# Turns of the identity ahead of three waits of TensorE in a four-layer transformer kernel

## The chip, the cores and the metric

The kernel runs on one core of one Trainium2 chip. The metric is the device time of one execution in microseconds, the median of the runs taken. The core has a matrix engine (TensorE, PE in the profile, with PEld for its weight loads), a vector engine (VectorE, DVE), an activation engine (ScalarE, ACT), GpSimd (POOL) and SyncE (SP), which starts the transfers. Each engine runs its own instructions in order and waits for the others by semaphores.

## The reference, cut to what matters

The activations x have the shape (2, 2048, 256) in float32. Four layers follow one another, each added to its input: an attention with 16 heads, a mixture, an attention by distance, and the same mixture again.

```python
x = x + attn_a(layernorm(x))                    # causal, 16 heads of 16
x = x + ffn(layernorm(x), Wr, W1, b1, W2, b2)
x = x + attn_b(layernorm(x), Wq, bq, Wk, bk, Wv, bv, Wo, bo)
x = x + ffn(layernorm(x), Wr, W1, b1, W2, b2)

def ffn(x, Wr, W1, b1, W2, b2):                 # 8 experts, the best 2 per batch
    top_scores, top_idx = top_k(x.mean(axis=1) @ Wr, 2)
    weights = softmax(top_scores)
    h = gelu(einsum('btd,bkdf->bktf', x, W1[top_idx]) + b1[top_idx])
    y = einsum('bktf,bkfd->bktd', h, W2[top_idx]) + b2[top_idx]
    return einsum('bk,bktd->btd', weights, y)

def attn_b(x, ...):                             # q, k, v are x @ W + b
    dist_sq = q_sq[:, :, None] + k_sq[:, None, :] - 2.0 * einsum('bqd,bkd->bqk', q, k)
    return einsum('bqk,bkd->bqd', softmax(exp(-dist_sq)), v) @ Wo + bo
```

## The kernel before

x stays on the core for the whole kernel, as 32 tiles of 128 rows. The work goes in stages: head attention, mixture 0, the weights of the distance attention, the distance attention, mixture 1. Between them stands a barrier of all engines, in most cases with a clearing of the stage's semaphores (`end_stage`, L106). A stage is written as one program for each engine; nothing plans it, the order within an engine is the order of the code.

A "turn" is a transpose on TensorE: a weight load and a matmul against the 128 x 128 identity, from on-chip memory into a bank of PSUM. Four turns bring two tiles of normed x into columns. A product in full precision is made of three matmuls, since each operand is split into a high and a low part: `split_product` (L634 to L636) multiplies high by high, low by high and high by low, 512 columns each.

**A mixture** (`mixture`) works on two batches of four chunks of 512 rows. A step is one of 2 experts x 8 slices of 128 hidden units: an "up" product of 6 matmuls (L634 to L636, into `f_h`), ScalarE's gelu (L912), VectorE's scaling by the gate and split into high and low (L983, L985), and a "down" product of 6 matmuls into `yps` (`f_ypsum`), three steps behind the up. The list `before` sets the head of the stage. All engines go through the same 14 entries in order and each does its part: 0 and 1 norm (VectorE, L606), 2 and 3 turn (TensorE, L617; ScalarE then copies the high part, L623), 4 and 5 low (VectorE, L628), 6 tanh (ScalarE, L893), 7 gate (VectorE, L945), 8 spread of the gates over the partitions (TensorE, L826), 9 gates (VectorE, L949), 10 turn of the biases (TensorE, L832), 11 biases (VectorE, L953 to L959, waits for entry 10), 12 and 13 the first two parts of the weights (ScalarE L902, then VectorE L965). TensorE's first up waits for VectorE's entry 12. Its third up (up 2) needs the third part of the weights, which ScalarE and VectorE make beside step 0, behind gelu 0. SyncE loads the raw weights from the start of the stage, in eight transfers of 512 KB, and for the first batch waits for nobody on TensorE.

**The distance attention** (`distance_attention`) begins with turns 0 and 1 (L1213), the projection (0, 0) and (0, 1) of q, turn 2, the projections (1, 0) and (1, 1) of k, the lengths, turn 3 and the values. The first projection needs the low halves of turns 0 and 1 (VectorE, L1468, behind ScalarE's high halves, L1349). `outs` are the four banks of the projections and results, of which bank 0 is first written for real by projection (0, 0). ScalarE takes each projection out twice (L1363 the value, L1366 its square). The 128 steps behind this head are scores, two exponentials and weighted values.

Of the kernel before, what the change touches and what calls it, by code (L numbers as in the profile page):

```python
# [40 lines left out]
P = 128  # L41
# [15 lines left out]
class Program:  # L57
# [36 lines left out]
    def ps(self, ctx):  # L94
        return lambda name, shape, dt: ctx.enter_context(self.nc.psum_tensor(name, shape, dt))
# [91 lines left out]
class Routing:  # L187
# [49 lines left out]
    def choose(self, dve):  # L237
        pr, b = self.pr, self.b
        dve.wait_ge(self.s_logit, 1)
        dve.tensor_copy(pr.logits[:], self.bank[0:1, 0:E]).then_inc(self.s_logits, 1)  # L240
        dve.wait_ge(self.s_logits, 1)
        dve.max(pr.best[:], pr.logits[:]).then_inc(self.s_best, 1)
        dve.wait_ge(self.s_best, 1)
        dve.max_index(pr.best_i[:, b, :], pr.best[:], pr.logits[:]).then_inc(self.s_chosen, 1)
        dve.tensor_tensor(pr.lead[0:1, b:b + 1], pr.best[0:1, 0:1], pr.best[0:1, 1:2], ALU.subtract).then_inc(self.s_chosen, 1)


def load_batch(pr, sp, b):
# [383 lines left out]
def split_product(pe, out, fixed_hi, fixed_lo, moving_hi, moving_lo, first, last):  # L632

    pe.matmul(out, fixed_hi, moving_hi, start=first, stop=False)  # L634
    pe.matmul(out, fixed_hi, moving_lo, start=False, stop=False)  # L635
    return pe.matmul(out, fixed_lo, moving_hi, start=False, stop=last)  # L636
# [35 lines left out]
def mixture(pr, layer, last_layer):  # L672
# [5 lines left out]
    with ExitStack() as ctx:  # L678
# [19 lines left out]
        yps = ps(f"{st}_ypsum", [P, 2 * KD, CHUNK], F32)  # L698
# [30 lines left out]
        def beside(n):  # L729
# [29 lines left out]
            if at < WP - ahead:  # L759
# [4 lines left out]
        before = [("norm", (0, 0)), ("norm", (0, 1)), ("turn", (0, 0)), ("turn", (0, 1)), ("low", (0, 0)), ("low", (0, 1)),  # L764
                  ("tanh", 0), ("gate", 0), ("spread", 0), ("gates", 0), ("turn_biases", 0), ("biases", 0)]
        before += [("weights", (0, i)) for i in range(AHEAD)]

        with nc.Block() as block:
# [30 lines left out]
            @block.tensor  # L799
            def _(pe):  # L800
                use = [0]
                side_reads = []

                def side_free():
                    for s_read, count in side_reads:
                        pe.wait_ge(s_read, count)
                    side_reads.clear()

                def do(kind, what):
                    if kind == "turn":  # L810
                        side_free()
                        cols.turn(pe, use[0])
                        use[0] += 1
                        return
                    if kind == "sums":
                        pe.wait_ge(cols.s_lo, use[0])
                        side_free()
                        routing.sums(pe)
                    elif kind == "logits":
                        routing.products(pe)  # L820
                        side_reads.append((routing.s_logits, 1))
                    elif kind == "spread":
                        pe.wait_ge(s_gate, what + 1)
                        pe.wait_ge(cols.s_lo, use[0])
                        side_free()
                        pe.matmul(side[:, 0:TOPK], pr.ones[0:1, :], gate[0:1, 4:4 + TOPK], start=True, stop=True).then_inc(s_spread, 1)  # L826
                        side_reads.append((s_gates, what + 1))
                    elif kind == "turn_biases":
                        pe.wait_ge(s_braw, 4 * 16 * (what + 1))
                        pe.wait_ge(cols.s_lo, use[0])  # L830
                        side_free()
                        pe.transpose(side[:, 0:BR], brow[:], pr.ident[0:BR, 0:BR]).then_inc(s_bturn, 1)  # L832
                        side_reads.append((s_bcol, what + 1))

                def up(n):
                    q, c, e, j = steps[n]
                    if c == 0:
                        pe.wait_ge(s_wl, WP * q + 8 * e + 2 * (j // 2) + 1)
                    if e == 0 and j == 0:
                        pe.wait_ge(cols.s_lo, (TILES // 2) * q + 2 * (c + 1))  # L840
                    if n >= 2:
                        pe.wait_ge(s_gelu, n - 1)
                    for k in range(KD):
                        mm = split_product(pe, hps[:, n % 2, :], w1h[:, e, k, j * P:(j + 1) * P], w1l[:, e, k, j * P:(j + 1) * P],
                                           cols.hi[:, k, c * CHUNK:(c + 1) * CHUNK], cols.lo[:, k, c * CHUNK:(c + 1) * CHUNK],
                                           k == 0, k == KD - 1)
                    mm.then_inc(s_h, 1)

                def down(n):
                    q, c, e, j = steps[n]  # L850
                    chunk = CHUNKS * q + c
                    if c == 0:
                        pe.wait_ge(s_wl, WP * q + 8 * e + 2 * (j // 2) + 2)
                    if e == 0 and j == 0 and chunk >= 2:
                        pe.wait_ge(s_y, KD * (chunk - 1))
                    pe.wait_ge(s_hl, n + 1)
                    for k in range(KD):
                        mm = split_product(pe, yps[:, KD * (chunk % 2) + k, :], w2h[:, e, j, k * P:(k + 1) * P],
                                           w2l[:, e, j, k * P:(k + 1) * P], hh[:, n % HR, :], hl[:, n % HR, :],
                                           e == 0 and j == 0, e == TOPK - 1 and j == FT - 1)  # L860
                    mm.then_inc(s_used, 1)

                for work in before:
                    do(*work)
                for n in range(len(steps) + LAG):
                    if n < len(steps):
                        up(n)
                    if n >= LAG:
                        down(n - LAG)
                    chunk, at = divmod(n, CS)  # L870
                    if 1 <= chunk < NB * CHUNKS and at in (4, 6):
                        add_tensor(pe, chunk - 1, (at - 4) // 2, ysb, s_y)
                    if n < len(steps):
                        for work in beside(n):
                            do(*work)
                for half in range(2):
                    add_tensor(pe, NB * CHUNKS - 1, half, ysb, s_y)
# [188 lines left out]
def distance_attention(pr, w):  # L1066
# [11 lines left out]
    with ExitStack() as ctx:  # L1078
# [24 lines left out]
        outs = ps("d_outs", [P, 2 * KD, CHUNK], F32)  # L1103
# [64 lines left out]
        def turn_bank(kind, p):  # L1168

            return {("turn", 1): banks[:, 0, :], ("turn", 2): banks[:, 1, :], ("values", 0): banks[:, 1, :]}.get((kind, p), turns[:])  # L1170
# [23 lines left out]
        with nc.Block() as block:  # L1194
            @block.tensor
            def _(pe):
# [7 lines left out]
                def turn(p):  # L1204
                    bank = turn_bank("turn", p)
                    if p not in (1, 2):
                        free(turn_read)
                        turn_read.append((s_xlo, p + 1))
                    pe.wait_ge(s_xn, 2 * p + 2)
                    out = bank.rearrange("p (k n) -> p k n", k=KD)  # L1210
                    for i in range(2):
                        for k in range(KD):
                            mm = pe.transpose(out[:, k, i * P:(i + 1) * P], xn[:, (2 * p + i) % 4, k * P:(k + 1) * P], pr.ident[:])  # L1213
                    mm.then_inc(s_turn, 1)
# [16 lines left out]
                def project(i, m):  # L1231
                    kind, g = tasks[i]
                    pe.wait_ge(s_xlo, 2 * g + 2)
                    if i in (7, 8, 14, 15):
                        pe.wait_ge(s_y, KD * {7: 1, 8: 3, 14: 4, 15: 5}[i])
                    elif i >= 2:
                        pe.wait_ge(s_lo, KD * (i - 1) + m + 1)
                    first = (2 * g % XR) * 2 * P
                    for k in range(KD):
                        mm = split_product(pe, outs[:, BANKS[i] + m, :], w.hi[kind][:, k, m * P:(m + 1) * P],  # L1240
                                           w.lo[kind][:, k, m * P:(m + 1) * P], xhi[:, k, first:first + CHUNK],
                                           xlo[:, k, first:first + CHUNK], k == 0, k == KD - 1)
                    mm.then_inc(s_p, 1)
# [63 lines left out]
                    mm.then_inc(s_rturned, 1)  # L1307

                do = {"turn": turn, "values": values, "project": project, "lengths": lengths}
                turn(0)  # L1310
                turn(1)
                project(0, 0)
                project(0, 1)
                turn(2)
# [5 lines left out]
                for n in range(STEPS + LAG):  # L1320
# [4 lines left out]
                    chunk, at = divmod(n, TILES)  # L1325
# [293 lines left out]
```

## Time and profile before

| what | value |
|---|---|
| median of 3 runs | 1852.38 us (1851.29 to 1853.46) |
| the profiled execution, its own time | 1851.4 us |
| its span, first to last instruction | 1849.4 us |
| TensorE busy | 1733.3 us, 94% of the span, 10063 matmuls |
| VectorE, ScalarE, GpSimd busy | 57%, 53%, 19% of the span |
| mean granted TensorE clock | 0.983 of full speed |

The profile is of one execution. Its times count from the first instruction; "granted clock" is the share of TensorE's full speed that the chip gave it, 1.00 for 2.4 GHz and 0.50 for 1.2 GHz. The ends of matmuls are modelled. A row's idle time is the time in which that engine did nothing ahead of the instruction, with the instruction that ended the wait.

### The profile page before, as it was taken

The page shows a single profiled execution, that of the slowest core. Times are in us where ns is not written, and L with a number is a line of the kernel's source. Part 1 is how long each engine was busy: PE and PEld are TensorE (multiplying, and loading weights), DVE is VectorE, ACT ScalarE, POOL GpSimd, SP SyncE. Part 2 cuts the span into 40 slices and gives each one's busy share as a digit, 9 for nine tenths or more (in the row PEclk, how much of TensorE's full clock was granted, in tenths as well). Part 3 has the DMA queues.
Part 4 walks back from the last instruction along what each step waited for, and adds up shares of the span by engine and source line. Part 5 has one row for each costly group of instructions (what it writes and reads, how often), then busy time and mean ns, then how long its engine had stood idle before and what let it go on. Part 6 is the DMA issues. An engine that isn't in the chain of part 4 may idle for free. (4 is left out here: it accounts for less than half of the span.)

```text
span 1849.4 us, 27445 instructions
## 1 busy us (share of the span) xinstructions
PE 1733.3 (94%) x10063; PEld 1138.5 (62%) x10063; DVE 1057.1 (57%) x2225; ACT 972.4 (53%) x1372; POOL 356.5 (19%) x466
## 2 busy tenths in 40 slices
PE   4999999999997999999998999999999799999998
PEld 1222222222222888888877887788788588888886
DVE  5443423444412775675546677865876587567554
ACT  3899999999996322332214544454444342233221
POOL 2222222232220000000003443533444200000000
PEclk9999999999998999999998999999999899999999
DMA  3000000000002002000000000000000200300000
GB/s 114 1 1 1 1 1 1 2 1 1 1 1 83 10 1 91 1 1 1 0 1 1 1 1 1 1 1 1 1 1 1 85 7 1 114 12 12 12 12 23
DMA packets 22912, 28.01 MB, mean 15 GB/s; under 512 B 1191, under 2 KB 18686, under 8 KB 22782
## 3 DMA queue, kind: packets, MB, share of 16 engines
q1 hardware_dynamic: 22782, 26.27, 4.3%
q8 instruction: 82, 1.34, 0.3%
q14 instruction: 48, 0.39, 0.1%
HBM read 22.07 MB, written 4.19 MB: 14 GB/s over the span
## 5 line engine op out<-in xcount | busy, mean ns | idle before, releaser
L449 ACT ACTIVATE a_probs<-a_scores 128x1024 f32<-128x1024 f32 (+3 forms) x640 | 513.0, 948 | 63.1 <-PE a_scores L549 61.3
L912 ACT ACTIVATE f_gelu<-f_h,f_bcol 128x512 f32<-128x512 f32 x256 | 176.6, 690 | 465.9 <-PE f_h L636 462.8
L527 PE MATMUL a_out<-a_probs,a_values 128*32 128x512 f32 (+3 forms) x2560 | 302.6, 545 | 4.4 <-POOL a_probs L472 4.3
L983 DVE TENSOR_SCALAR f_hh<-f_gelu,f_gates 128x512 fp32r<-128x512 f32 x256 | 124.3, 486 | 242.0 <-ACT f_gelu L912 240.8
L549 PE MATMUL a_scores<-a_moving,a_fixed 64*128 64x512 f16 (+3 forms) x1280 | 195.5, 355 | 29.8 <-ACT a_probs L449 22.4
L634 PE MATMUL f_h<-f_xhi,f_w1h 128*128 128x512 f32 x512 | 208.5, 407 | 11.3 <-DVE f_w1l L965 11.3
L1399 ACT ACTIVATE d_score<-d_dist,d_nksq 128x512 f32<-128x512 f32 x128 | 92.8, 725 | 213.7 <-DVE d_dist L1543 213.7
L636 PE MATMUL f_h<-f_xhi,f_w1l 128*128 128x512 f32 x512 | 202.2, 395 | 0.0
L635 PE MATMUL f_h<-f_xlo,f_w1h 128*128 128x512 f32 x512 | 201.8, 394 | 0.0
L634 PE MATMUL f_ypsum<-f_hh,f_w2h 128*128 128x512 f32 x512 | 199.8, 390 | 0.0
L636 PE MATMUL f_ypsum<-f_hh,f_w2l 128*128 128x512 f32 x512 | 199.5, 390 | 0.0
L635 PE MATMUL f_ypsum<-f_hl,f_w2h 128*128 128x512 f32 x512 | 199.4, 389 | 0.0
L985 DVE SCALAR_TENSOR_TENSOR f_hl<-f_gelu,f_gates,f_hh 128x512 fp32r<-128x512 f32 x256 | 192.4, 752 | 9.2
L549 PEld LDWEIGHTS a_scores<-a_moving,a_fixed 64*128 64x128 f16 x1280 | 47.7, 94 | 230.7 <-ACT a_probs L449 194.1
L1439 POOL TENSOR_TENSOR distance_raw<-distance_raw,d_p 128x512 f32<-128x512 f32 x112 | 145.4, 1298 | 201.0 <-ACT d_p L1373 200.9
L472 POOL TENSOR_SCALAR_AFFINE_SELECT a_probs<-a_probs 128x256 f32<-128x256 f32 x256 | 101.1, 410 | 247.3 <-ACT a_probs L449 243.4
L1543 DVE SCALAR_TENSOR_TENSOR d_dist<-d_banks,d_qsq 128x512 f32<-128x512 f32 x128 | 88.0, 687 | 63.6 <-PE d_banks L636 63.4
L634 PEld LDWEIGHTS f_h<-f_xhi,f_w1h 128*128 128x128 f32 x512 | 97.7, 191 | 31.3 <-DVE f_w1l L965 13.1
L636 PEld LDWEIGHTS f_h<-f_xhi,f_w1l 128*128 128x128 f32 x512 | 97.5, 190 | 21.3
L527 PEld LDWEIGHTS a_out<-a_probs,a_values 128*32 128x32 f32 x2560 | 50.6, 108 | 97.0 <-issue 83.0
L635 PEld LDWEIGHTS f_h<-f_xlo,f_w1h 128*128 128x128 f32 x512 | 98.0, 191 | 18.2
L636 PEld LDWEIGHTS f_ypsum<-f_hh,f_w2l 128*128 128x128 f32 x512 | 96.3, 188 | 20.4
(186 smaller groups left out, 2613.7 us busy)
## 6 DMA issues: line engine op xcount, KB each, us to landing
f_raw<-in_L_ffn_W SPq DMA_DIRECT2D x32, 512.0 KB, 7.5
x<-in_L_attn_a_x SPq DMA_DIRECT2D x8, 512.0 KB, 7.2
out<-x SPq DMA_DIRECT2D x8, 512.0 KB, 2.9
distance_raw<-in_L_attn_b_Wv SPq DMA_DIRECT2D x1, 256.0 KB, 7.0
distance_raw<-in_L_attn_b_Wo SPq DMA_DIRECT2D x1, 256.0 KB, 6.5
distance_raw<-in_L_attn_b_Wq SPq DMA_DIRECT2D x1, 256.0 KB, 6.6
distance_raw<-in_L_attn_b_Wk SPq DMA_DIRECT2D x1, 256.0 KB, 6.5
f_brow<-in_L_ffn_b SPq DMA_DIRECT2D x8, 4.0 KB
```

The lines of the kernel that those rows point to most:

```text
L449: act.activation(probs[:, u % UR, :, 0:w], scores[:, 2 * (u % SR):2 * (u % SR) + 2, 0:w], ACT.Exp, scale=HD ** -0.5).then_inc(s_exp, 1)
L472: pool.affine_select(out=tri, in_=tri, compare_op=ALU.is_ge, fill=0.0, base=0, pattern=[[0, 2], [1, P]], channel_multiplier=-1).then_inc(s ...
L527: mm = pe.matmul(spare[32 * j:32 * j + 32, i % 2, skip:CHUNK], values[:, G % 2, kt, j, :], probs[:, (2 * n + j // 2) % UR, j % 2, 0:w], st ...
L549: mm = pe.matmul(scores[:, 2 * (u % SR) + h, 0:w], fixed[head, G % 2, a, kt * P:(kt + 1) * P], moving[head, G % 2, a, q0:q0 + w], start=Tr ...
L634: pe.matmul(out, fixed_hi, moving_hi, start=first, stop=False)
L635: pe.matmul(out, fixed_hi, moving_lo, start=False, stop=False)
L636: return pe.matmul(out, fixed_lo, moving_hi, start=False, stop=last)
L912: act.activation(gel[:, n % HR, :], hps[:, n % 2, :], ACT.Gelu, bias=bcol[:, q, FT * e + j:FT * e + j + 1])\
L983: dve.tensor_scalar(hh[:, n % HR, :], gel[:, n % HR, :], gates[:, q, e:e + 1], None, ALU.mult).then_inc(s_hh, 1)
L985: dve.scalar_tensor_tensor(out=hl[:, n % HR, :], in0=gel[:, n % HR, :], scalar=gates[:, q, e:e + 1], in1=hh[:, n % HR, :].bitcast(F32), op ...
L1399: act.activation(score[:, n % 2, :], dist[:, n % DR, :], ACT.Exp, scale=-1.0, bias=nksq[:, b, kt:kt + 1]).then_inc(s_score, 1)
L1439: pool.tensor_tensor(acc, acc, p32[:, n % R, :], ALU.add).then_inc(s_acc, 1)
```

## The change

A new helper, `idle_turns`, issues a number of turns of the identity into a bank. It waits for nothing and signals nothing. In each mixture TensorE issues 20 such turns ahead of entry 0 of `before`, 20 ahead of entry 9 (so between the spread and the turn of the biases), and 24 behind the list, ahead of the first up. They go into bank 0 of `yps`, which the first down product starts anew. In the distance attention it issues 14 ahead of turn 0 and 12 between turn 1 and the first projection, into bank 0 of `outs`, which that projection starts anew. The result is the same.

```diff
--- before.py
+++ after.py
@@ -243,6 +243,12 @@
         dve.wait_ge(self.s_best, 1)
         dve.max_index(pr.best_i[:, b, :], pr.best[:], pr.logits[:]).then_inc(self.s_chosen, 1)
         dve.tensor_tensor(pr.lead[0:1, b:b + 1], pr.best[0:1, 0:1], pr.best[0:1, 1:2], ALU.subtract).then_inc(self.s_chosen, 1)
+
+
+def idle_turns(pr, pe, bank, count):
+
+    for _ in range(count):
+        pe.transpose(bank[:, 0:P], pr.ident[:], pr.ident[:])
 
 
 def load_batch(pr, sp, b):
@@ -860,8 +866,11 @@
                                            e == 0 and j == 0, e == TOPK - 1 and j == FT - 1)
                     mm.then_inc(s_used, 1)
 
-                for work in before:
+                for at, work in enumerate(before):
+                    if at in (0, 9):
+                        idle_turns(pr, pe, yps[:, 0, :], 20)
                     do(*work)
+                idle_turns(pr, pe, yps[:, 0, :], 24)
                 for n in range(len(steps) + LAG):
                     if n < len(steps):
                         up(n)
@@ -1307,8 +1316,10 @@
                     mm.then_inc(s_rturned, 1)
 
                 do = {"turn": turn, "values": values, "project": project, "lengths": lengths}
+                idle_turns(pr, pe, outs[:, 0, :], 14)
                 turn(0)
                 turn(1)
+                idle_turns(pr, pe, outs[:, 0, :], 12)
                 project(0, 0)
                 project(0, 1)
                 turn(2)
```

## Rows read from the trace of the kernel before

**Rows 1.** The page, parts 1 and 2: busy times, granted clock in 40 slices.
```profile
PE 1733.3 (94%) x10063; PEld 1138.5 (62%) x10063; DVE 1057.1 (57%) x2225; ACT 972.4 (53%) x1372; POOL 356.5 (19%) x466
...
PEclk9999999999998999999998999999999899999999
```

**Rows 2.** Timeline, first mixture's head: start us, us, engine, line, operation, [idle before].
```profile
585.70 1.38 DVE L606 TENSOR_SCALAR f_xn<-x,mv,rstd 128x256 f32<-128x256 f32 x4 [0.99 <-PEq L106]
586.49 0.66 PE L617 MATMUL f_side<-ident,f_xn 128*128 128x128 f32 x4 [2.99 <-DVE f_xn L606]
587.14 1.03 PE L617 MATMUL f_misc<-ident,f_xn 128*128 128x128 f32 x4
...
589.67 0.55 PE L826 MATMUL f_side<-f_gate,ones 1*128 1x2 f32 x2 [1.50 <-DVE f_gate L945]
...
594.34 0.80 PE L634 MATMUL f_h<-f_xhi,f_w1h 128*128 128x512 f32 x1 [3.51 <-DVE f_w1l L965]
...
597.35 1.28 ACT L912 ACT_TABLE_LOAD   x1 [2.15 <-PE f_h L636]
...
601.62 0.79 PE L634 MATMUL f_h<-f_xhi,f_w1h 128*128 128x512 f32 x1 [2.79 <-DVE f_w1l L965]
```

**Rows 3.** One-microsecond windows, first mixture: length, busy times; PEclk third from last.
```profile
587.00:588.00 1.00, 1.00 (x6) 0.63 (x4) 0.27 (x2) 0.60 (x1) 0.00 (x0) 0.64 0.00 0
...
597.00:598.00 1.00, 1.00 (x5) 0.74 (x4) 0.00 (x0) 0.65 (x1) 0.00 (x0) 0.74 1.02 370
...
600.00:601.00 1.00, 0.00 (x0) 0.00 (x0) 1.00 (x3) 0.95 (x2) 0.00 (x0) 0.96 1.05 378
...
607.00:608.00 1.00, 1.00 (x4) 0.76 (x3) 0.64 (x2) 0.85 (x2) 0.00 (x0) 0.62 0.00 0
```

**Rows 4.** Timeline in narrow windows: two turns at full, two and three at low clock.
```profile
586.49 0.44 PE L617 MATMUL f_side<-ident,f_xn 128*128 128x128 f32 x2 [2.99 <-DVE f_xn L606]
...
1464.74 0.69 PE L617 MATMUL f_side<-ident,f_xn 128*128 128x128 f32 x2 [2.79 <-DVE f_xn L606]
...
1464.74 0.90 PE L617 MATMUL f_side<-ident,f_xn 128*128 128x128 f32 x3 [2.79 <-DVE f_xn L606]
```

**Rows 5.** Timeline, head of the distance attention.
```profile
979.37 2.20 DVE L1463 TENSOR_SCALAR d_xn<-x,mv,rstd 128x256 f32<-128x256 f32 x4 [0.32 <-PEq L1012]
...
980.16 1.12 PE L1213 MATMUL d_turns<-ident,d_xn 128*128 128x128 f32 x4 [1.88 <-DVE d_xn L1463]
...
981.62 1.12 PE L1213 MATMUL d_banks<-ident,d_xn 128*128 128x128 f32 x4 [0.35 <-DVE d_xn L1463]
...
984.15 0.80 PE L634 MATMUL d_outs<-d_xhi,wq_hi 128*128 128x512 f32 x1 [1.41 <-DVE d_xlo L1468]
...
989.44 0.79 PE L1213 MATMUL d_banks<-ident,d_xn 128*128 128x128 f32 x3
```

**Rows 6.** One-microsecond windows, head of the distance attention.
```profile
979.00:980.00 1.00, 0.00 (x0) 0.00 (x0) 0.68 (x3) 0.00 (x0) 0.14 (x1) 0.90 0.00 0
...
990.00:991.00 1.00, 1.00 (x7) 0.87 (x6) 0.00 (x0) 1.00 (x3) 0.00 (x0) 0.98 0.00 0
```

**Rows 7.** Timeline, head of the second mixture.
```profile
1464.74 1.12 PE L617 MATMUL f_side<-ident,f_xn 128*128 128x128 f32 x4 [2.79 <-DVE f_xn L606]
...
1468.22 0.55 PE L826 MATMUL f_side<-f_gate,ones 1*128 1x2 f32 x2 [1.50 <-DVE f_gate L945]
...
1472.27 0.80 PE L634 MATMUL f_h<-f_xhi,f_w1h 128*128 128x512 f32 x1 [2.89 <-DVE f_w1l L965]
...
1479.55 0.49 PE L634 MATMUL f_h<-f_xhi,f_w1h 128*128 128x512 f32 x1 [1.80 <-DVE f_w1l L965]
...
1482.40 0.39 PE L634 MATMUL f_ypsum<-f_hh,f_w2h 128*128 128x512 f32 x1
```

**Rows 8.** One-microsecond windows, head of the second mixture.
```profile
1461.00:1462.00 1.00, 0.95 (x4) 0.55 (x4) 0.01 (x1) 0.00 (x0) 0.00 (x0) 0.54 0.00 0
...
1478.00:1479.00 1.00, 0.00 (x0) 0.00 (x0) 1.00 (x3) 1.00 (x2) 0.00 (x0) 0.92 1.05 375
```

## The prediction

> **What bounds the kernel now.** The page comes first: TensorE is busy for 94% of the span, and its granted clock dips in only a few of the forty slices [rows 1]. In the long middle of each stage one matmul follows another, so a delay or a gain at a stage's head reaches the end of the kernel almost whole, and the change can only matter at three heads. I read those with two views: the timeline, for who starts when, and the one-microsecond windows, for the granted clock. Times such as 586.49 are microseconds from the span's start.
>
> At the head of the first mixture the reader is to see short pieces of work that wait for VectorE and for the weights: two groups of four turns, the spread of the gates, and only at 594.34 the first product (up 0), then a wait to 601.62 before up 2 [rows 2]. The clock falls to half speed (1.2 GHz) at about 587.3. It rises to 2.4 GHz at about 597.5, falls again at about 600.9 and rises at about 607.8 [rows 3]. At the distance attention's head the clock falls at 979.8 and rises at 990.0 [rows 6], over the first twelve projections, which take 5.3 us from 984.15 to 989.44 [rows 5], 0.44 each. At full speed twelve products take 2.85, from 1479.55 to 1482.40 [rows 7], 0.24 each. Before the second mixture it has fallen at 1461.1, ahead of the stage, and rises at 1478.1 [rows 7, 8].
>
> What half speed costs there, as a ceiling: products run in it for 3.2 and 6.1 us in the first mixture, 5.9 in the distance attention, and 5.5 in the second mixture (1472.27 to 1477.75, where the 1.80 us of idle time ahead of 1479.55 begin). Full speed would halve each, 10.3 us in all. That is the most there is to win.
>
> **The price of one turn.** Two turns take 0.44 us and four take 0.66 at the full clock, so a further one costs 0.11. At the low clock two take 0.69 and three 0.90, so 0.21 [rows 2, 4]. Twenty cost 2.2 or 4.2 us, 24 cost 2.6 or 5.0, 14 cost 1.5 or 2.9, 12 cost 1.3 or 2.5. The change adds 2 x 64 + 26 = 154 turns. All stand in TensorE's own order, in front of real work, so each turn beyond the pause it stands in makes that work late. Nobody reads the bank before its first real write, which starts it anew, so nobody waits for the turns themselves.
>
> **First mixture.** When TensorE comes out of the stage's barrier isn't shown. The bounds are 585.70, VectorE's first instruction, and 586.49, TensorE's own first [rows 2]; I take 586.0. The pause that the first 20 turns are to fill is then 0.5 us. Twelve run before the clock falls at 587.3, as it did, and 8 at 0.21, so they end at 589.0. The eight real turns follow, a group of four at 1.1 us and one at 0.9, and end near 591.0 against 588.17, so 2.8 late. ScalarE's copies, VectorE's lows, the tanh and the gate hang on them, so the spread moves from 589.67 to 592.5. Behind it come 20 turns, the turn of the biases, and 24 turns, before up 0. VectorE's wait for the biases now stands behind the first 20, and VectorE makes its first half of the weights only after that wait; even so this half comes before the 24 have ended, so the turns are what is late. Those 44 take 4.8 us at the full clock. From the low clock it depends on when the clock rises: the four stretches of products above saw it rise 3.2, 5.9, 5.8 and 6.1 us after they began. With 3.2 the 44 take 15 x 0.21 + 29 x 0.11 = 6.4; with 6.1 they take 29 x 0.21 + 15 x 0.11 = 7.8. I take 6.4, between the others. With 0.7 for the spread (0.55 [rows 2]) and the one turn of the biases, up 0 starts at 599.6, 5.3 late (3.7 to 6.7). It then runs at full speed and is done after 1.55 us (6 x 0.24 and the end of the last) instead of 3.0 (from 594.34 to ScalarE's table load at 597.35 [rows 2]), which gives back 1.45. What follows is a chain: table load, gelu 0, VectorE's next weights, up 2 at 601.62. It is not shortened, so it starts 3.8 later. Up 1 ends with the same pause of some 3 us behind it, in which the clock fell before. I take the same fall again, so nothing is gained there; the other end is a clock that holds, for half of 6.1 us. First mixture: **+3.8**, from -0.9 to +5.2.
>
> **Distance attention.** VectorE starts at 979.37, and I let TensorE go into its 14 turns at 979.4. The clock fell at 979.8. TensorE had then been idle since 978.28, of the 1.88 us ahead of its first turn [rows 5, 6]. The pause shrinks to 1.1. The nearest row is the pause of 1.80 us ahead of 1479.55, over which the clock stood at full speed [rows 7, 8], so I take it that it holds. Turn 0 then starts at 980.9, 0.75 late, but takes 0.66 for 1.12, and ends at 981.6 against 981.28. Turn 1 ends at 982.2 against 982.74. The twelve turns end at 983.5, just ahead of the low halves, due 1.4 us behind turn 1 as before, at 983.6. So they are hidden, and the projections start at 983.6 for 984.15. The twelve projections take 2.85 us for 5.3, and turn 2 comes at 986.5, 2.9 early. ScalarE and VectorE, which copy each projection as it ends, follow it. **-2.9**. The ends are -3.2 (half of 5.3, and the 0.55 of the earlier start), and +2.4 if the clock is low throughout and the projections simply begin at 986.5 behind turns at 0.21.
>
> **Second mixture.** The same code, but the clock is low on arrival. Twenty turns from 1464.2 take 4.2 us, so the real ones start at 1468.4, 3.7 late, and end 2.8 to 3.7 late; I take 3.2. The spread goes from 1468.22 to 1471.4 [rows 7]. The 44 turns take 4.8, 6.4 or 7.8 as above, and up 0 starts 4.6, 6.2 or 7.6 late, less the 1.45 that up 0 gains. Here the clock was at full speed from 1478.1 already, and nothing is left to gain behind. I take **+4.7**, from +3.2 to +9.3, the upper end with a second fall during the pause before up 2, for half of 6.1 us.
>
> **Sum.** 3.8 - 2.9 + 4.7 = +5.6 us. The profiled execution took 1851.4 us (span 1849.4 and 2.0 around it), 1.0 below the median of 1852.38. That gives 1857.0 on its own time and 1858.0 on the median; I predict 1857.5. A measurement of this kernel can tell about 0.2%, 3.7 us, from no change; the forecast lies just beyond.
>
> **Rivals.** *Turns do not raise the clock (15%).* For it: the eight turns from 980.16 did not bring the clock up, and it rose only 5.9 us after the projections had begun [rows 5, 6]. Against it: they had waits between them, the eight of the second mixture as well, and no row shows turns back to back for microseconds. Every added turn outside the first 1.3 us then costs 0.21. First mixture: the 44 take 9.2 us and up 0 starts at 602.4, 8.1 late and at its old speed. Distance attention: 2.4 late in half speed, some +1.8. Second mixture: 3.7 late at the turns, then 0.7 + 9.2 against a gap of 4.05 from spread to up 0, +9.5. Sum +19.4, so 1871. The Trainium skill says this of its own accord: "TensorE: Matmul & The Clock Gate", Part 4 (PE-mode transpose), has it that a transpose does not count as busy for the clock as a product does and that full speed does not engage for it. By that rule the time is this rival's; no run here shows it yet.
>
> *The clock never falls: faster (11%).* The place is the barrier before each mixture: if the first 20 turns bridge it, they run at 0.11. First mixture: they end at 588.2, the real turns at 589.2 (+1.0), up 0 at 596.2 (+1.8), less 1.45, less 3.1 for a clock that holds at 600.9: -2.8. Second mixture: real turns end 0.8 late, 0.7 + 4.8 against the gap of 4.05, less 1.45: +0.8. With the distance attention's -2.9 the sum is -4.9, so 1847. It decides only if both mixtures' barriers are bridged; with the second one's clock low on arrival, as it is now, that mixture costs +3.2 and the sum is -2.5, no change that can be told. Against it: both pauses are about 3 us long before a turn can start, and the clock fell before or within them.
>
> *Nothing comes of it (6%).* The turns are dropped, or losses and gains cancel: 1852.
>
> **Chances.** The forecast has 68%, the three rivals 15, 11 and 6. Within the forecast the ends run from about +1 (the low end in one mixture) to +11; I give its own range as 1853 to 1863. For 8 in 10 the range reaches over the cancelling case, and above over the forecast's upper end to a clock that rises late in both mixtures: 1850 to 1866. What is left out is the first rival, most of the second at its full price, and little else. Slower by over 0.2%: 0.53 of the forecast's 0.68 and the 0.15 of the first rival, 0.68. Within 0.2%: 0.13 of the forecast, whose low third lies under 3.7 us, the 0.06 of the cancelling case and 0.01 of the second rival, 0.20. Faster: 0.02 of the forecast and 0.10 of the second rival, 0.12.
>
> **What would show it.** TensorE has 10217 matmuls for 10063. Right: in the first mixture up 0 lies 13.9 us behind VectorE's first instruction of the stage, where it lay 8.6 behind (585.70 to 594.34); the twelve first projections take 2.9 us; up 0 of the second mixture comes 6 us later in its stage, its products spaced 0.24. Wrong: up 0 within 2 us of its old place, turns spaced 0.21 through all 44 (the first rival), or a granted clock of 1.00 from 582 to 620 (the second). The forecast fails if TensorE is free much before VectorE after a barrier, or if the delay at a mixture's head is taken up by slack behind it that I don't see.

## The result, and the profile after

The changed kernel takes 1854.78 us (median of 20 runs; before 1851.91 in the same measurement). The ratio is 1.0015, with a 95% interval of 1.0008 to 1.0021: slower by 2.8 us, 1.5 to 3.9 (the two medians differ by 2.9). That is clear of zero and below the 0.2% from which the prediction counted. One execution of 8153.7 us is left out of the ratio; the others lie between 1851.2 and 1857.9. The profiled execution took 1854.2 us, with a span of 1852.4, 3.0 more than before. The helper and its calls move the lines by 6 to 11, so L251 is the new helper and L634 to L636 have become L640 to L642.

The page of the changed kernel, parts 1 and 2, to be read against [rows 1]:

```profile
PE 1745.8 (94%) x10217; PEld 1153.2 (62%) x10217; DVE 1057.5 (57%) x2225; ACT 972.4 (52%) x1372; POOL 356.5 (19%) x466
...
PEclk9999999999999999999999999999999999999999
```

There are 154 matmuls more, as announced. No slice shows the clock below nine tenths any more, though more time passes: the clock was bought, and it cost more than it gave.

**First mixture.** Timeline of TensorE in the changed kernel, the counterpart of [rows 2]:

```profile
585.94 2.38 PE L251 MATMUL f_ypsum<-ident 128*128 128x128 f32 x20 [2.20 <-PEq L106]
588.15 0.60 PE L623 MATMUL f_side<-ident,f_xn 128*128 128x128 f32 x4
588.59 0.60 PE L623 MATMUL f_misc<-ident,f_xn 128*128 128x128 f32 x4
590.85 0.35 PE L832 MATMUL f_side<-f_gate,ones 1*128 1x2 f32 x2 [1.67 <-DVE f_gate L954]
591.13 2.40 PE L251 MATMUL f_ypsum<-ident 128*128 128x128 f32 x20
...
593.63 2.84 PE L251 MATMUL f_ypsum<-ident 128*128 128x128 f32 x24
596.23 0.47 PE L640 MATMUL f_h<-f_xhi,f_w1h 128*128 128x512 f32 x1
...
602.21 0.79 PE L640 MATMUL f_h<-f_xhi,f_w1h 128*128 128x512 f32 x1 [2.98 <-DVE f_w1l L974]
```

and the one-microsecond windows, the counterpart of [rows 3]:

```profile
587.00:588.00 1.00, 1.00 (x12) 1.00 (x10) 0.33 (x2) 0.00 (x0) 0.00 (x0) 1.00 0.00 0
...
601.00:602.00 1.00, 0.00 (x0) 0.00 (x0) 1.00 (x3) 0.54 (x2) 0.00 (x0) 0.58 1.10 359
```

TensorE is free at 585.94, in the same moment as VectorE, and 20 turns take 2.38 us: the clock did not fall at 587. The real turns end at 589.2 against 588.17; as this stage starts 0.24 later, they are 0.8 us late in it. The 20, the turn of the biases and the 24 take 5.1 us at full speed. Up 0 lies 10.29 us behind VectorE's first instruction of the stage for 8.64 before, and up 2 16.27 for 15.92. The clock then fell in the wait ahead of up 2 (at 601.2, to 608.0), as it had before.

**Distance attention.** The counterpart of [rows 5]:

```profile
979.68 1.72 PE L251 MATMUL d_outs<-ident 128*128 128x128 f32 x14 [1.08 <-PEq L1021]
981.24 0.60 PE L1222 MATMUL d_turns<-ident,d_xn 128*128 128x128 f32 x4
981.96 0.66 PE L1222 MATMUL d_banks<-ident,d_xn 128*128 128x128 f32 x4
982.45 1.47 PE L251 MATMUL d_outs<-ident 128*128 128x128 f32 x12
984.03 0.50 PE L640 MATMUL d_outs<-d_xhi,wq_hi 128*128 128x512 f32 x1
...
986.88 0.60 PE L1222 MATMUL d_banks<-ident,d_xn 128*128 128x128 f32 x4
```

Turn 2 is 7.20 us into its stage for 10.07 before (VectorE starts at 979.68 and started at 979.37): 2.87 us gained. Further on something is given back. This is a wait of TensorE in the changed kernel, 302 us into the stage, with two windows behind it:

```profile
1281.64 1.05 PE L1263 MATMUL d_misc<-ones,distance_raw 128*128 128x1 f32 x8 [1.48 <-DVE x L1526]
...
1283.00:1284.00 1.00, 1.00 (x6) 0.82 (x5) 0.00 (x0) 0.00 (x0) 0.00 (x0) 0.91 0.00 0
...
1287.00:1288.00 1.00, 1.00 (x5) 0.77 (x5) 0.00 (x0) 0.00 (x0) 0.74 (x1) 0.88 0.00 0
```

and the same wait in the kernel before (it ends when VectorE has read a result), with the window that lies within it:

```profile
1284.44 1.05 PE L1254 MATMUL d_misc<-ones,distance_raw 128*128 128x1 f32 x8 [1.48 <-DVE x L1515]
...
1283.00:1284.00 1.00, 0.00 (x0) 0.00 (x0) 1.00 (x3) 0.82 (x2) 0.10 (x1) 1.00 0.08 16
```

In the kernel before the clock stood over that wait. In the changed one, where the wait ended at 1281.6, it fell 2.2 us behind it, for 3.4 us, in products.

**Second mixture.** The counterpart of [rows 7], and of [rows 8] below it:

```profile
1462.34 4.50 PE L251 MATMUL f_ypsum<-ident 128*128 128x128 f32 x20 [1.99 <-PEq L106]
1466.64 1.06 PE L623 MATMUL f_side<-ident,f_xn 128*128 128x128 f32 x4
1467.49 0.93 PE L623 MATMUL f_misc<-ident,f_xn 128*128 128x128 f32 x4
1469.92 0.35 PE L832 MATMUL f_side<-f_gate,ones 1*128 1x2 f32 x2 [1.50 <-DVE f_gate L954]
1470.20 2.41 PE L251 MATMUL f_ypsum<-ident 128*128 128x128 f32 x20
...
1472.70 2.84 PE L251 MATMUL f_ypsum<-ident 128*128 128x128 f32 x24
1475.30 0.48 PE L640 MATMUL f_h<-f_xhi,f_w1h 128*128 128x512 f32 x1
...
1481.29 0.50 PE L640 MATMUL f_h<-f_xhi,f_w1h 128*128 128x512 f32 x1 [2.99 <-DVE f_w1l L974]
```

```profile
1461.00:1462.00 1.00, 0.00 (x0) 0.00 (x0) 0.27 (x1) 0.00 (x0) 0.00 (x0) 0.66 0.00 0
...
1468.00:1469.00 1.00, 0.42 (x3) 0.15 (x1) 0.63 (x1) 0.88 (x3) 0.00 (x0) 0.93 0.99 344
...
1481.00:1482.00 1.00, 0.71 (x3) 0.58 (x4) 0.96 (x3) 0.00 (x0) 0.00 (x0) 0.90 0.00 0
...
1485.00:1486.00 1.00, 1.00 (x6) 0.81 (x5) 0.96 (x3) 0.11 (x2) 0.00 (x0) 0.89 0.00 0
```

Here the first 20 turns take 4.50 us at the low clock. Up 0 is 12.95 us into the stage for 8.32 before, and up 2 18.94 for 15.60. Half a microsecond behind the start of up 2 the clock falls, at 1481.8, and rises at 1485.2; before, it stood there.

The ledger, each stage from VectorE's first norm in it to that of the next, the last one to the end of the span, in the profiled executions:

| kernel | first mixture and distance weights | distance attention | second mixture |
|---|---|---|---|
| before | 393.67 | 484.58 | 385.47 |
| changed | 393.74 (+0.1) | 482.67 (-1.9) | 390.10 (+4.6) |

With +0.2 from the head attention, which the change doesn't touch, this is the +3.0 of the spans.

### The profile page after: what moved, and what is told of

It reads as the page before. It is cut to its first block and busy times, and to the rows that moved or that the text cites. A ratio compares the mean times of both kernels' runs of the same rounds, so it can differ in the third digit from the quotient of the medians.

```text
span 1852.4 us, 27753 instructions
## 1 busy us (share of the span) xinstructions
PE 1745.8 (94%) x10217; PEld 1153.2 (62%) x10217; DVE 1057.5 (57%) x2225; ACT 972.4 (52%) x1372; POOL 356.5 (19%) x466
## 5 line engine op out<-in xcount | busy, mean ns | idle before, releaser
L640 PE MATMUL f_h<-f_xhi,f_w1h 128*128 128x512 f32 x512 | 207.3, 405 | 6.0 <-DVE f_w1l L974 6.0
L642 PE MATMUL f_h<-f_xhi,f_w1l 128*128 128x512 f32 x512 | 201.4, 393 | 0.0
L640 PE MATMUL f_ypsum<-f_hh,f_w2h 128*128 128x512 f32 x512 | 199.8, 390 | 0.0
L642 PE MATMUL f_ypsum<-f_hh,f_w2l 128*128 128x512 f32 x512 | 199.6, 390 | 0.0
L640 PEld LDWEIGHTS f_h<-f_xhi,f_w1h 128*128 128x128 f32 x512 | 97.2, 190 | 25.0 <-DVE f_w1l L974 6.8
L642 PEld LDWEIGHTS f_h<-f_xhi,f_w1l 128*128 128x128 f32 x512 | 96.9, 189 | 21.1
L642 PEld LDWEIGHTS f_ypsum<-f_hh,f_w2l 128*128 128x128 f32 x512 | 96.1, 188 | 20.5
L641 PEld LDWEIGHTS f_ypsum<-f_hl,f_w2h 128*128 128x128 f32 x512 | 96.3, 188 | 20.2
```

## The experiments

Each kernel was timed in five rounds against the kernel before, on the same chip; the first four shared one chip, e5 to e8 a second and e9 and e10 a third. A difference from the kernel before is worked out from the ratio. A difference between two kernels with turns is that of their medians; where the ratios say something else by more than 0.5 us, they stand beside it. The diffs are against the kernel named, and the parts of no weight are left out: the helper in e1, and in e2 and e3 the writing of the condition on `at` as a table of counts. Theory A is the one that the profiles suggest: a turn costs its 0.11 or 0.21 us where it stands ahead of work that is ready, and gives what the clock gives. Theory B is that the result is scatter from where the clock falls inside the stages.

**The distance attention alone.**

```diff
--- before
+++ e1
+                idle_turns(pr, pe, outs[:, 0, :], 14)
                 turn(0)
                 turn(1)
+                idle_turns(pr, pe, outs[:, 0, :], 12)
                 project(0, 0)
```

> Only the 14 and 12 turns of the distance attention, none in the mixtures. Theory A (what a turn costs is its place in TensorE's order; what it brings is clock): turn 2 comes 2.9 us earlier in its stage, and 1.5 to 3 us of that reach the end, so 0.1% faster than before, near 1849.5. Theory B (turns bring nothing or little, and the 2.9 us by which the changed kernel is slower are scatter from where the clock happens to fall in the middle of the stages): within 1 us of before.

Measured: 1849.13 us, ratio 0.9986 (0.9977 to 0.9995), 2.6 us faster (0.9 to 4.3). Turn 2 came 7.20 us into its stage, as in the changed kernel, and the stage took 482.5 us for 484.6. So the 26 turns there are a gain, as A had it.

**The mixtures alone.**

```diff
--- after
+++ e2
-                idle_turns(pr, pe, outs[:, 0, :], 14)
...
-                idle_turns(pr, pe, outs[:, 0, :], 12)
```

> Only the 20, 20 and 24 turns of each mixture, none in the distance attention. Theory A: slower than before by the changed kernel's 2.9 us and the 2 to 3 us that the distance attention no longer gives, so by 4.5 to 6 us, near 1857. Up 0 starts 10.3 us behind the first norm in the first mixture, up 2 of the second mixture 3 us later in its stage. Theory B: +2.9 as the whole change, or less.

Measured: 1857.42 us, ratio 1.0027 (1.0017 to 1.0036), 5.0 us slower (3.2 to 6.7; the medians differ by 5.8). Within these intervals the parts add up: 5.0 - 2.6 is 2.4, and the whole was 2.8. B falls for the mixtures. Up 0 of the first mixture was at 11.8 us and not at 10.3, since here the clock fell during the first 20 turns, which took 3.38 us for 2.38:

```profile
585.18 3.38 PE L251 MATMUL f_ypsum<-ident 128*128 128x128 f32 x20 [2.20 <-PEq L106]
588.36 1.06 PE L623 MATMUL f_side<-ident,f_xn 128*128 128x128 f32 x4
589.21 0.89 PE L623 MATMUL f_misc<-ident,f_xn 128*128 128x128 f32 x4
```

So the same code up to this point met a clock that stood in one execution and fell in another, and the +0.1 of the changed kernel's profile is not what every execution shows: here the first mixture and the distance weights took 395.3 us, 1.6 more than before. The second mixture took 390.1, as in the changed kernel, but by another way. The clock fell at 1473.8, within the 44 turns, though TensorE did one turn after another:

```profile
1473.04 3.81 PE L251 MATMUL f_ypsum<-ident 128*128 128x128 f32 x20
...
1475.00:1476.00 1.00, 1.00 (x6) 1.00 (x5) 0.00 (x0) 0.00 (x0) 0.00 (x0) 0.50 1.09 361
```

Up 0 came at 14.3 us and up 2 at 20.3, for 13.0 and 18.9 in the changed kernel, and then the clock stood over the wait ahead of up 2.

**The wait ahead of up 2.**

```diff
--- after
+++ e3
                     if n < len(steps):
                         up(n)
+                    if n == 1:
+                        idle_turns(pr, pe, yps[:, 0, :], 24)
```

> The whole change, and 24 more turns in each mixture between up 1 and up 2, where TensorE waits 3 us for the weights. At 0.11 us each they take 2.6 us and end inside the wait. Theory A: the clock no longer falls before up 2, which saves 2.4 us in the first mixture (up 2 to up 4 took 6.9 us at a low clock and 4.7 at a high one) and 1.3 in the second: 3.7 us faster than the changed kernel, near 1851. Theory B: 48 more turns cost or change nothing, 1854 to 1855.

Measured: 1851.73 us, ratio 1.0000 (0.9991 to 1.0009), 3.1 us less than the changed kernel, as A had it. The profile shows where in part: from up 2 to up 4 now took 4.7 us in both mixtures, for 6.9 and 5.8 in the changed kernel. But this profiled execution is the slowest of its eleven and only 0.8 us shorter than the changed kernel's. The clock was low twice at both heads (585.8 to 589.2 and 592.6 to 596.0; 1459.6 to 1466.4 and 1469.8 to 1473.2), the second time within the 44 turns, so up 2 came at 19.6 and 20.2 us for 16.3 and 18.9, the first mixture took 395.4 us and the second 390.0. The distance attention took 481.0, with no fall at 1283.

**Turns cut to the waits.**

```diff
--- after
+++ e4
                 for at, work in enumerate(before):
-                    if at in (0, 9):
-                        idle_turns(pr, pe, yps[:, 0, :], 20)
+                    idle_turns(pr, pe, yps[:, 0, :], {0: 4, 8: 6}.get(at, 0))
                     do(*work)
-                idle_turns(pr, pe, yps[:, 0, :], 24)
+                idle_turns(pr, pe, yps[:, 0, :], 16)
...
+                    if n == 1:
+                        idle_turns(pr, pe, yps[:, 0, :], 24)
```

> Turns cut to the waits: in each mixture 4 ahead of the first turn, 6 ahead of the spread, 16 ahead of up 0, 24 behind up 1, and the 14 and 12 of the distance attention. Even at 0.21 us each they fit the waits of 0.8, 1.5, 3.5 and 3 us (at 0.11 the last one). Theory A: up 0 starts within 0.3 us of its old place in both mixtures and runs at full speed (-1.4 each in the chain through gelu 0), the clock holds before up 2 (-2.4 in the first mixture), distance attention -1.9 to -2.9: 7 to 8 us faster than before, near 1844.5. If so few turns at the low clock don't bring it up in time, up 0 and up 1 run at half speed and it is 4 to 5 us faster. Theory B: within 2 us of before.

Measured: 1844.07 us, ratio 0.9954 (0.9941 to 0.9968), some 8 us faster. Its timeline at the head of the second mixture:

```profile
1457.86 1.09 PE L251 MATMUL f_ypsum<-ident 128*128 128x128 f32 x4 [1.99 <-PEq L106]
1458.73 1.06 PE L623 MATMUL f_side<-ident,f_xn 128*128 128x128 f32 x4
1459.59 1.06 PE L623 MATMUL f_misc<-ident,f_xn 128*128 128x128 f32 x4
1460.44 1.49 PE L251 MATMUL f_ypsum<-ident 128*128 128x128 f32 x6
1462.15 0.56 PE L832 MATMUL f_side<-f_gate,ones 1*128 1x2 f32 x2 [0.23 <-DVE f_gate L955]
1463.05 0.26 PE L838 MATMUL f_side<-ident,f_brow 20*128 20x20 f32 x1 [0.34 <-DVE f_gates L959]
1463.25 3.68 PE L251 MATMUL f_ypsum<-ident 128*128 128x128 f32 x16
1466.57 0.71 PE L640 MATMUL f_h<-f_xhi,f_w1h 128*128 128x512 f32 x1
1467.12 0.39 PE L641 MATMUL f_h<-f_xlo,f_w1h 128*128 128x512 f32 x1
...
1469.68 2.78 PE L251 MATMUL f_ypsum<-ident 128*128 128x128 f32 x24
1472.80 0.50 PE L640 MATMUL f_h<-f_xhi,f_w1h 128*128 128x512 f32 x1 [0.34 <-DVE f_w1l L975]
```

Every group of turns ends close to where the next real work becomes ready. The first three groups of turns ran at the low clock; up 0 came at 8.7 us into the stage for 8.3 before, but with the clock up from its second matmul on. Up 2 came at 14.9 us for 15.6 before. Together with the clock held behind up 1 this is 384.8 us for the stage, 0.7 less than before and 5.3 less than with the changed kernel's counts. The first mixture took 389.9 us, 3.7 less than before, and the distance attention 482.7, 1.9 less, as in the changed kernel.

**Without the first 20.**

```diff
--- after
+++ e5
                 for at, work in enumerate(before):
-                    if at in (0, 9):
-                        idle_turns(pr, pe, yps[:, 0, :], 20)
+                    idle_turns(pr, pe, yps[:, 0, :], {9: 20}.get(at, 0))
```

> The whole change without the first 20 turns of each mixture (20 and 24 stay, and the distance attention's). Theory A: the real turns come 0.8 us earlier in the first mixture and 3.3 in the second, but the 44 turns then begin at a low clock and take 6.4 to 7.8 us instead of 5.3, so up 0 starts within 2 us of the changed kernel's place in either; 1853.5 to 1856, no more than 1.5 us from the changed kernel. Theory C (the first 20 are what costs: they push the real turns, the rest is hidden): 4 us faster than the changed kernel, near 1850.5.

Measured: 1852.84 us, ratio 1.0003 (0.9994 to 1.0012), 1.9 us less than the changed kernel. This lies between A's bound of 1.5 and C's 4, so A's size was missed. The profile shows A's mechanism: the real turns came at their old place, and the next 20 turns took 4.18 us in the first mixture (3.94 in the second) instead of 2.40, since the clock was low. Up 0 lay at 11.4 us in both mixtures, for 10.3 and 13.0. To leave out the first 20 thus gives back some 1.9 of the 5.0 us that the mixtures lose. What the 44 cost alone is the step from e1 to this kernel, which differ in nothing else: 3.7 us by the medians, 3.1 by the ratios.

**Without the turns behind up 1.** The fitted kernel without its last edit.

```diff
--- e4
+++ e6
-                    if n == 1:
-                        idle_turns(pr, pe, yps[:, 0, :], 24)
```

> The fitted kernel (1844.1) without the 24 turns behind up 1. Theory A: in the wait of 3 us before up 2 the clock falls again in most executions; up 2 to up 4 take 6.9 us at a low clock for 4.7, and the second mixture loses 1.3 to 2.3: 3 to 4.5 us slower than the fitted kernel, near 1848, still faster than before. If the clock stays up over this wait because it was raised later, 1844 to 1845.

Measured: 1845.22 us, ratio 0.9964 (0.9950 to 0.9978), 1.1 us more than the fitted kernel by the medians and 1.9 by the ratios, for the 3 to 4.5 that were expected, and the two intervals overlap. Its profile holds both cases, with the same wait of 3.0 us ahead of up 2. The clock stood over it in the first mixture (window 599) and fell in the second (window 1473):

```profile
599.00:600.00 1.00, 0.21 (x1) 0.21 (x2) 1.00 (x3) 0.12 (x1) 0.00 (x0) 1.00 1.04 379
...
1473.00:1474.00 1.00, 1.00 (x4) 0.81 (x3) 0.78 (x2) 0.00 (x0) 0.00 (x0) 0.50 0.48 155
```

In the profiles of the four kernels with waits of 3.0 us here, eight in all, up 2 to up 4 took 4.7 us twice (the clock stood) and 5.8 to 6.9 six times. So the length of the wait alone doesn't decide whether it costs. That it also differs from execution to execution of one kernel is likely, as the clock's falls moved between executions of the same code above, but no kernel was profiled twice.

**Products in place of turns.**

```diff
--- e4
+++ e7
-        pe.transpose(bank[:, 0:P], pr.ident[:], pr.ident[:])
+        pe.matmul(bank[:, 0:P], pr.ident[:], pr.ident[:], start=True, stop=True)
```

> The fitted kernel with each turn of the identity replaced by a plain product of the identity with itself, same place, same count. Theory A (for the clock a turn counts as any matmul does): the same time within 0.7 us, near 1844, and the clock rises at the same places. Theory D (turns count for less than products): the clock rises earlier or falls less often with products, 1 to 3 us faster.

Measured: 1853.02 us, ratio 1.0004 (0.9995 to 1.0013), 9 us more than the fitted kernel. Both theories missed, for a reason in the form. Groups of TensorE in this kernel:

```profile
L251 PE MATMUL f_ypsum<-ident 128*128 128x128 f32 x200 | 25.5, 287 | 4.2 <-PEq L106 4.2
...
L251 PE MATMUL d_outs<-ident 128*128 128x128 f32 x52 | 6.2, 276 | 0.8 <-PEq L1022 0.8
```

There were 100 and 26 calls: a product in float32 is two matmuls, and each pair took 0.22 us at the full clock (48 matmuls in 5.3 us). The 24 behind up 1 took 5.5 us in a wait of 3, and up 2 came at 16.6 and 18.1 us for 14.5 and 14.9. That is A's price of overrun once more, and no test of the clock. So half as many:

```diff
--- e7
+++ e9
-                    idle_turns(pr, pe, yps[:, 0, :], {0: 4, 8: 6}.get(at, 0))
+                    idle_turns(pr, pe, yps[:, 0, :], {0: 2, 8: 3}.get(at, 0))
...
-                idle_turns(pr, pe, yps[:, 0, :], 16)
+                idle_turns(pr, pe, yps[:, 0, :], 8)
...
-                        idle_turns(pr, pe, yps[:, 0, :], 24)
+                        idle_turns(pr, pe, yps[:, 0, :], 12)
...
-                idle_turns(pr, pe, outs[:, 0, :], 14)
+                idle_turns(pr, pe, outs[:, 0, :], 7)
...
-                idle_turns(pr, pe, outs[:, 0, :], 12)
+                idle_turns(pr, pe, outs[:, 0, :], 6)
```

> The fitted kernel with products in place of turns, but half as many (2, 3, 8 and 12 in each mixture, 7 and 6 in the distance attention), since the profile of the products showed that each became two matmuls and took 0.23 us for 0.11. TensorE is then occupied as long as in the fitted kernel. Theory A (turns count for the clock as products do, and the 8 us that the first trial lost were overrun): 1843.5 to 1845. Theory D (products count for more): below 1843. If products are bad for another reason than their length, it stays near 1850.

Measured: 1844.82 us, ratio 0.9959 (0.9945 to 0.9972), the fitted kernel's time within 1 us, and the clock was low for some 41 us of the profiled execution in both. For the clock, a turn is worth as much here as a product that occupies TensorE as long.

**Five more waits.** First all of them, then only the two inside the distance attention.

```diff
--- e4
+++ e8
-                for half in range(2):
+                for half, count in ((0, 12), (1, 7)):
+                    idle_turns(pr, pe, hps[:, 0, :], count)
                     add_tensor(pe, NB * CHUNKS - 1, half, ysb, s_y)
+                idle_turns(pr, pe, hps[:, 0, :], 8)
...
                     for kind, *what in AT.get(n, ()):
+                        if kind == "lengths" and n in (55, 71):
+                            pe.wait_ge(s_dist, n)
+                            idle_turns(pr, pe, banks[:, (n + 1) % 2, :], {55: 24, 71: 12}[n])
```

The added wait is for VectorE to have read the bank that the turns write. The other kernel, e10, has the second of these edits alone.

> The fitted kernel with turns in five more waits: 12, 7 and 8 at the end of each mixture (the stage of the distance weights behind the first one ran at a low clock), 24 in the wait of 2.9 us and 12 in the wait of 1.5 us inside the distance attention, at about 1197 and 1281 us, where the clock fell in all and in half of the profiles. Theory A: 1.5 us from the distance weights, 1.7 to 2.4 from the wait at 1197, 0.8 on average from the one at 1281: 4 to 5 us faster than the fitted kernel, near 1839.5. Theory B (falls inside a stage are absorbed by slack behind them): 1842 to 1844.

> The fitted kernel with only the 24 and 12 turns inside the distance attention added, none at the end of the mixtures. Theory A: the clock no longer falls at 1197 and 1281; 2.5 to 4.5 us faster than the fitted kernel (1844.1), near 1840.5, so most of what the kernel with all five fills gained (1838.8). Theory E (the gain was at the ends of the mixtures): 1843 to 1844.

Measured: 1838.75 us, ratio 0.9927 (0.9914 to 0.9941) with all five, and 1841.31, ratio 0.9944 (0.9930 to 0.9957) with the two. The two inside save 2.8 us by the medians, 1.9 by the ratios, and the distance attention takes 479.5 us for 482.7. In the changed kernel TensorE waited 2.87 us there:

```profile
1194.04 0.60 PE L1315 MATMUL d_misc<-ident,d_y 128*128 128x128 f32 x4
1197.52 1.05 PE L1263 MATMUL d_misc<-ones,distance_raw 128*128 128x1 f32 x8 [2.87 <-DVE x L1526]
```

and in e10 24 turns fill the wait:

```profile
1190.26 0.60 PE L1316 MATMUL d_misc<-ident,d_y 128*128 128x128 f32 x4
1190.70 2.78 PE L251 MATMUL d_banks<-ident 128*128 128x128 f32 x24
1193.75 1.05 PE L1264 MATMUL d_misc<-ones,distance_raw 128*128 128x1 f32 x8 [0.27 <-DVE x L1530]
```

In e10's distance attention the clock stood from the first turn to the last microsecond; in all ten profiles without these fills it fell between 1194 and 1202, for 3.4 or 6.8 us. So the falls inside the stage reached the end, against B. Of the further 2.6 us of e8 (3.1 by the ratios) the profiles show only 0.4 at the end of the first mixture: the clock still fell at 968.8, at the first wait of the distance weights. But e8's profile is of its slowest execution, 1840.9 us with a mean clock of 0.992. In three of the other four the mean clock was 0.996 or 0.997, which no execution of e10 had (0.990 to 0.992). So in most of its executions the clock was low for less time still; an estimate from these means (0.004 to 0.005 of 1838 us, doubled, since the low clock counts half) is 15 to 18 us less. Which of the falls were missing there isn't shown. With 1838.75 us e8 is the best version, 0.73% faster than the kernel before.

## Why the prediction was right or wrong

**Direction and size.** Slower was forecast and slower it was, by 2.8 us for the 5.6 forecast. The time of 1854.8 lies in the range, near the lower end of the forecast's own. "Slower by over 0.2%" had the largest chance; 0.15% falls under "within 0.2%", which had 0.20.

**The price of a turn** was right: 24 turns moved the next work by 2.60 us (593.63 to 596.23), forecast 2.6, and 20 at the low clock by 4.30 (1462.34 to 1466.64), forecast 4.2.

**First mixture**, forecast +3.8, came out at +0.1 in the profile and +1.6 to +1.7 in e2 and e3. The step that failed is "Twelve run before the clock falls at 587.3, as it did". The moment of a fall was taken from one execution and carried over to another kernel with other work in it. In the changed kernel's profile the clock stood from the first turn to the wait ahead of up 2, so the 20 turns delayed the real ones by 0.8 us and not 2.8, and the 44 took 5.1 us and not 6.4. In e2 it fell within the first 20 turns but was back at 589.8, ahead of the 44: up 0 came at 11.8 us, forecast 13.9. In e3 it fell within the 20 and again within the 44, and there the forecast's steps came nearly true: up 0 at 13.6, and up 2 at 19.6, forecast 19.7. The sign of the term and its chain (up 0 late, some of it given back by its full speed, the same chain to up 2) held in all of them; what came back was 1.3 us, forecast 1.45.

**Distance attention**, forecast -2.9: the head gave 2.87, step by step as forecast. What the step "reaches the end of the kernel almost whole" left out are the waits inside the stage. In the changed kernel's profile a wait of 1.5 us at about 1281, over which the clock had stood, was followed by a fall; the stage kept 1.9. In e3, where it wasn't, it kept 3.5, some 0.7 more than the head had given; where that came from isn't shown. Timed alone, the 26 turns gave 2.6 (e1).

**Second mixture**, forecast +4.7 and +4.6 in the profile. That they agree so closely is in part luck, since two terms missed and made up for each other. The first 20 turns cost what was said (the real ones 3.3 us late at their end). The clock rose at 1468.1, with nothing but turns done since 1462.34, and so the 44 took 5.1 us instead of 6.4: up 0 was 4.6 late and not 6.2, up 2 3.3 and not 4.7. The missing 1.2 came from the second fall, just behind the start of up 2, which the forecast had put at the upper end. In e2 and e3, where the clock fell again within the 44, these took 6.7 us, and the forecast's own steps came true: up 0 at 14.3 and 14.2 us (forecast 14.5), up 2 at 20.3 and 20.2 (forecast 20.3). In e2 the clock then stood over the wait, as forecast. So here again the clock took different ways in different executions, and the forecast had described one of them.

**The rivals.** *Turns do not raise the clock* falls, by the rise at 1468.1 and by e9 against e4. With it falls, for this kernel, the rule of the Trainium skill that was set beside it ("TensorE: Matmul & The Clock Gate", Part 4): here back-to-back turns of float32 raised the clock, and in the changed kernel's profile it stood through the 20 and the 44 of the first mixture. They are no safeguard, as the falls within the 44 in e2 and e3 show. *The clock never falls* came about half: it held over the first mixture's barrier in the changed kernel's profile, but not in e2 or e3, and over the second's in none, and the deciding point named, both barriers, was not reached.

**What the forecast did not see** is that its own reasoning held a much better kernel. It priced each turn that overruns its wait, and the waits were in the rows: 0.8, 1.5 and 3.5 us. Turns cut to them, with 24 more in the wait ahead of up 2, turned +2.8 into about -8.

## What to carry to other kernels

Filler work on an engine is free only up to the end of the wait it stands in, so count it at its price at the low clock. Look for the waits in the whole timeline: those inside a busy stage cost too, as soon as the clock falls behind them (two of them some 3 us here). And take the moment of a fall or a rise of the clock from several executions, since it moved by microseconds between them and decided terms of 1 to 3 us.

## What the runs showed of the hardware

- The clock's fall is not a matter of the length of a wait alone. Over waits of 3.0 us ahead of up 2, in four kernels and both mixtures, it stood twice and fell six times. The wait of 1.48 us inside the distance attention was followed by a fall in four profiles (the changed kernel, e1, e4, e9) and not in the six others that left it unfilled. A fall can come after the wait is over, in dense work: 2.2 us behind the wait's end at 1283.8 in the changed kernel, 0.8 us into back-to-back turns at 1473.8 in e2.
- Turns of the identity (float32, 128 x 128) count for the clock as products do, as far as these runs show. After it had fallen at 1461.3, turns alone from 1462.34 brought it back at 1468.1, 5.8 us later. Put in place of such turns, products that occupied TensorE as long left the kernel's time the same within 1 us.
- A float32 product of 128 x 128 by 128 columns is issued as two matmuls and takes 0.22 us at the full clock, twice the 0.11 of a transpose of the same size.
